# Ordering a graph by TensorE counts, with x scattered and layer 0's rows made beside the neighbour lists

## The chip, the cores and the metric

One NeuronCore of a Trainium2 chip runs the kernel as one program. The metric is the device time of a launch in microseconds (us), the median of several executions. The engines are named as the profile names them: PE is TensorE (matmul), DVE VectorE, ACT ScalarE, POOL GpSimd, SP SyncE, which here only issues DMAs. PS is the accumulator memory behind PE (eight banks of 512 floats in each of 128 partitions), `big` is one large SBUF buffer out of which nearly all tiles are cut by hand.

## What is computed

Four graph attention layers, each behind a layer norm with a relu and in front of a residual add, on x of 8 x 2048 x 64 (batch, nodes, features). The graph is sparse: a node has itself and about four neighbours on average.

```python
h = jnp.maximum(_layernorm(x, axis=-1), 0.0)
x = x + _L0_gnn_ref(h, adj, L0_gnn_W, L0_gnn_a, L0_gnn_gamma, L0_gnn_beta)
h = jnp.maximum(_layernorm(x, axis=-1), 0.0)
x = x + _L1_gnn_ref(h, adj, ...)      # 4 heads of h h^T scores, then a second attention
h = jnp.maximum(_layernorm(x, axis=-1), 0.0)
x = x + _L2_gnn_ref(h, adj, ...)      # query/key/value attention
h = jnp.maximum(_layernorm(x, axis=-1), 0.0)
x = x + _L3_gnn_ref(h, adj, L3_gnn_W, L3_gnn_a)

def _L0_gnn_ref(h, adj, W, a, gamma, beta):
    Wh = jnp.einsum('bnf,fo->bno', h, W)
    e = (Wh @ a[:Fout] + jnp.swapaxes(Wh @ a[Fout:], 1, 2)) / dk
    e = jax.nn.leaky_relu(e, negative_slope=0.2)
    attention = jax.nn.softmax(jnp.where(adj[None] > 0, e, NEG_INF), axis=2)
    h_prime = jnp.einsum('bij,bjo->bio', attention, Wh)
    # batch norm per node over batch and features, gamma, beta, then + h, then elu
```

## The kernel before

Nodes are worked in NT = 16 tiles of P = 128; a node's row holds its E = 512 numbers (8 batches of 64 features). The kernel first sorts the nodes by degree, so that a tile has as many neighbour slots as its largest node needs (SLOTS, 87 slots in all, between 2 and 13 in a tile). Every attention layer then gathers, for each tile and slot, the 128 rows of that neighbour with one indirect DMA that POOL issues (`gather`, L654, 71 a layer), and DVE, ACT and PE score, weigh and add them. If a node does not fit its slots, a flag sends all engines to another, dense program (`far_away`), which these inputs do not take; the other branch is `near`.

Everything up to the first gather is the part at issue here, and no engine's order there is set by a planner: each engine's program is written out by hand and runs in that order, with semaphores between them.

1. Masks. SP loads adj in 16 tiles into three buffers (L504). For each tile DVE writes a 0/1 mask in fp16 and its row sums, the degrees (L1489), and takes the diagonal out (L1491, L1493).
2. Ranks. DVE makes a key of degree and node number (L1497 to L1500); SP stores it and loads it back broadcast to all partitions (L507, L509). Meanwhile DVE clears and fills the weight tiles (L1502 to L1531). The rank of a node is the number of keys above its own: ACT counts for ten tiles by a sign with a running sum (L824), DVE for six by a comparison (L1535). Thirteen small operations turn ranks into places (L1542 to L1548).
3. Places. SP stores the places and loads them back broadcast (L512, L514), DVE casts them (L1558). ACT then issues the 16 loads of x (L833).
4. Lists. For each tile the mask is multiplied by the places, by POOL for 12 tiles (L638) and by DVE for four (L1568); five MAX8 and more on DVE take the largest places out as the neighbour list (L1570 to L1577). Lists, gamma, beta, bias and node number are written into the same row XR as x (547 numbers). Then the flag is made (L1587 to L1595).
5. Scatter. POOL sends the 16 tiles of XR to their places in the DRAM tensor xs by indirect DMAs (L644). SP loads lists and x back in order (L550, L552).
6. Layer 0's rows. `norm(0, s)` runs over DVE, POOL and ACT (sum and mean L1608 and L1609, centring L666, square L854, sum L1613, Ln and Exp L858 and L861, relu and scale L1617 into H0). PE turns each tile by four transposes (L1176), ACT takes it out (L845), PE multiplies it with the weights (`half`, L1196), ACT takes that out (L872), SP stores it into tab0 (L530), from which the gathers read.

In layer 0 itself the loop of m runs on each engine: `add_up` on PE adds the weighed slots of a tile (L1214), POOL gathers tile m + 2 once `summed` says that tile m - 2 is done, DVE does `weigh` (L1675), `add_terms` and `lower`, `elu_add` (L1739, L1741), `norm(1, ...)`, `elu_low` (L1732, L1733, which adds H0) and `bn_stats`.

## Time and profile before

| | us |
|---|---|
| median of 3 runs | 1794.92 (1794.16 to 1799.05) |
| the profiled execution, its own time | 1795.05 |
| its span in the profile | 1793.2 |
| busy: DVE, PE, POOL, ACT | 1308.8, 1080.2, 1035.0, 784.8 |
| mean granted clock of TensorE | 0.858 |

The granted clock is a share of full speed: 1.00 is the level of 2.4 GHz and 0.50 that of 1.2 GHz. All times within the profile count from the start of the span. A PE record of a matmul on float32 stands for half of the instruction: the 87 slot sums of a layer give 174 records, and `half` gives eight records for a tile's four matmuls, while a transpose is one record. "x16" behind an instruction is how many are merged in a row, and the text in square brackets is how long the engine had been idle and what ended it.

### The profile page before, as it was taken

Reading aid. Unit: us, or ns where it says so; the run is one execution under the profiler, and the core shown is the slowest. Engines: PE = TensorE matmul, PEld = TensorE weight load, DVE = VectorE, ACT = ScalarE, POOL = GpSimd, SP = SyncE. Lnnn points to the kernel's source line nnn. Section 1 sums busy time; section 2 is a strip of 40 time slices with the busy share of each in tenths; the row PEclk is TensorE's granted clock in tenths of the full one; section 3 lists DMA queues with packets and bytes.
Section 4 is the critical chain, followed back from the end, with each engine's and each line's share of the span. In section 5 each row is a group of like instructions: output and inputs, shape, how many; then the busy total and the mean of one; then the engine's idle time right before and its main releaser. Section 6 shows DMA issues by size and latency. Waiting matters only on the chain.

```text
span 1793.2 us, 13782 instructions
## 1 busy us (share of the span) xinstructions
PE 1080.2 (60%) x3144; PEld 558.8 (31%) x3144; DVE 1308.8 (73%) x1699; ACT 784.8 (44%) x2502; POOL 1035.0 (58%) x939
## 2 busy tenths in 40 slices
PE   0000255365289899869999985646534777764673
PEld 0000132122144444434444441212113444542231
DVE  7987456789699997994768505999976986734462
ACT  0400253334247566544655652536433546643131
POOL 0084437641167788657686656877744865415882
PEclk9999988687699899979999998877775889876886
DMA  9260547431222122101111004442204543206666
GB/s 339 74 117 20 198 153 207 136 114 48 94 62 80 41 66 64 53 12 30 42 41 36 12 12 143 131 114 84 87 24 138 149 137 96 70 34 186 199 186 160
DMA packets 101626, 178.81 MB, mean 100 GB/s; under 512 B 47552, under 2 KB 56032, under 8 KB 99232
## 3 DMA queue, kind: packets, MB, share of 16 engines
q0 software_dynamic: 30960, 102.92, 19.9%
q1 hardware_dynamic: 51216, 70.05, 11.8%
q10 hardware_dynamic: 19360, 4.87, 1.6%
q8 instruction: 28, 0.46, 0.1%
q14 instruction: 62, 0.51, 0.1%
HBM read 147.88 MB, written 34.12 MB: 101 GB/s over the span
## 4 chain that ended last, share of the span: by engine, by line
DVE 30%; PE 29%; POOL 19%; issue 11%; ACT 5%; DMA 4%; DVEq 0%; POOLq 0%; ACTq 0%; SPq 0%
PE PS L1230 15%; POOL big L654 10%; DVE big L1691 5%; DVE big L1683 3%; PE PS L1176 3%; PE PS L1254 2%; PE PS L1290 2%; ACT big L897 2%; PE PS L1242 2%; DVE big L1687 2%; DVE big L1570 2%; POOL big L682 2%; DVE big L1617 2%; DVE stats L1613 2%; DVE big L1489 2%
## 5 line engine op out<-in xcount | busy, mean ns | idle before, releaser
L1230 PE MATMUL PS<-big,ident 128*128 128x512 f32 x1044 | 507.5, 637 | 107.1 <-ACT big L897 45.2
L897 ACT ACTIVATE big<-big 128x64 f32<-128x64 f32 x1632 | 404.7, 339 | 241.8 <-DVE big L1648 202.6
L682 POOL TENSOR_TENSOR big<-big 128x512 f32<-128x512 f32 x356 | 361.5, 1045 | 134.8 <-DVE big L1648 113.0
L1230 PEld LDWEIGHTS PS<-big,ident 128*128 128x128 f32 x1044 | 209.7, 206 | 367.4 <-issue 269.4
L1691 DVE TENSOR_REDUCE big<-big 128x32 f32<-128x2048 f32 (+4 forms) x126 | 297.7, 2362 | 4.3
L1214 PE MATMUL PS<-big,ident 128*128 128x512 f32 x348 | 190.3, 708 | 153.7 <-ACT big L897 85.8
L1683 DVE TENSOR_TENSOR big<-big,PS 128x2048 f32<-128x2048 f32 (+4 forms) x84 | 198.5, 2363 | 80.9 <-PE PS L1242 78.1
L654 POOL DMA_INDIRECT big<-tab,SI x142 | 174.2, 1227 | 117.7 <-PE PS L1214 40.9
L1176 PE MATMUL PS<-ident,big 128*128 128x128 f32 x640 | 105.8, 295 | 167.8 <-DMA big<-h_rows 67.8
L689 POOL TENSOR_TENSOR big<-big 128x512 f32<-128x512 f32 x64 | 81.5, 1273 | 147.7 <-ACT big L970 147.3
L654 POOL DMA_INDIRECT big<-h_rows,SI x142 | 138.4, 974 | 44.7 <-issue 27.2
L1214 PEld LDWEIGHTS PS<-big,ident 128*128 128x128 f32 x348 | 77.3, 229 | 265.6 <-issue 232.0
L1176 PEld LDWEIGHTS PS<-ident,big 128*128 128x128 f32 x640 | 82.8, 151 | 236.3 <-DMA big<-h_rows 69.4
L1687 DVE TENSOR_TENSOR big<-big,PS 128x2048 f32<-128x2048 f32 (+4 forms) x42 | 99.3, 2363 | 68.2 <-DMA big<-h_table,SI 56.8
L666 POOL TENSOR_TENSOR big<-big,stats 128x512 f32<-128x512 f32 x64 | 66.7, 1043 | 106.4 <-DVE stats L1609 106.2
L638 POOL TENSOR_TENSOR big<-big 128x2048 f16<-128x2048 f16 x12 | 51.1, 4294 | 98.8 <-DVE big L1558 96.1
L1613 DVE TENSOR_REDUCE stats<-big 128x8 f32<-128x512 f32 x64 | 43.9, 686 | 78.8 <-ACT big L854 77.1
L879 ACT ACTIVATE big<-big 128x40 f32<-128x40 f32 (+12 forms) x80 | 20.2, 253 | 176.5 <-DVE big L1637 176.5
L1242 PE MATMUL PS<-MB,big 128*128 128x256 f32 x256 | 67.5, 411 | 34.9 <-DVE big L1683 22.3
L654 POOL DMA_INDIRECT big<-h_table,SI x71 | 70.3, 990 | 25.4 <-issue 17.7
L854 ACT ACTIVATE big<-big 128x512 f32<-128x512 f32 x64 | 40.0, 625 | 101.7 <-POOL big L666 101.7
L1675 DVE TENSOR_TENSOR big<-big 128x2048 f32<-128x2048 f32 (+6 forms) x32 | 77.7, 2428 | 1.1
(159 smaller groups left out, 1534.7 us busy)
## 6 DMA issues: line engine op xcount, KB each, us to landing
big<-in_adj SPq DMA_DIRECT2D x16, 1024.0 KB, 6.1
tab<-big SPq DMA_DIRECT2D x64, 132.0 KB, 1.8
big<-tab SPq DMA_DIRECT2D x32, 264.0 KB, 3.3
h_rows<-big SPq DMA_DIRECT2D x32, 256.0 KB, 2.0
big<-h_rows SPq DMA_DIRECT2D x32, 256.0 KB, 2.8
big<-in_x ACTq DMA_DIRECT2D x16, 256.0 KB, 5.0
big<-xs SPq DMA_DIRECT2D x4, 1024.0 KB, 9.4
h_table<-big SPq DMA_DIRECT2D x16, 256.0 KB, 2.0
```

The source lines that it names most:

```text
L654: pool.indirect_dma_start(out=rowbuf[t % NRB][:, k * w:(k + 1) * w], out_offset=None, in_=tables[u], in_offset=bass.IndirectOffsetOnAxis(a ...
L682: ins = pool.tensor_tensor(bd(wbuf[:, i % NWB, j, :]), bd(rows[:, k + j, :]), over_d(S[:, h, k + j, :], B), ALU.mult)
L689: pool.tensor_tensor(zA[:, j % 2, :], zA[:, j % 2, :], zB[:, j % 2, :], ALU.add).then_inc(z_added, 1)
L897: ins = act.activation(to, row, ACT.Copy, scale=S[:, h, k + j, b:b + 1])
L1176: mm = pe.transpose(to[:, q * P:(q + 1) * P], rows[:, q * P:(q + 1) * P], ident[:, :])
L1214: mm = pe.matmul(to.rearrange("p (b d) -> p b d", b=B), ident[:, :], rows[:, k, :].rearrange("p (b c) -> p b c", b=B)[:, :, 0:D], start=(k ...
L1230: mm = pe.matmul(to, ident[:, :], wbuf[:, i % NWB, k, :], start=(u != 2 and c == 0 and k == 0), stop=(c == len(parts) - 1 and k == n - f - 1))
L1242: mm = pe.matmul(bank(4 + 2 * hp + q // 2)[:, (q % 2) * 256:(q % 2 + 1) * 256], hTo[:, t % 2, q * P:(q + 1) * P], MB[:, 2 * hp:2 * hp + 2, ...
L1613: tell(dve.tensor_reduce(stats[:, 2, v], bd(sqn[:, n % 2, :]), AX.X, ALU.add), var_made, n + 1)
L1683: return dve.tensor_tensor(pr.rearrange("p k (q c) -> p k q c", q=4), rows.rearrange("p k (q c) -> p k q c", q=4), q_half(h // 2, h).unsqu ...
L1687: return dve.tensor_tensor(pr, rows, mine.unsqueeze(1).to_broadcast([P, n, E]), ALU.mult)
L1691: run(dve.tensor_reduce(scores(u, t)[:, h, k:k + n, :].rearrange("p k b -> p (k b)"), bd(prod[:, 0:n * E]), AX.X, ALU.add))
```

## The change

- Ranks. Each node's degree becomes a one-hot vector of NV = 32 classes (L1648 of the changed kernel, a 128 x 512 fp16 tile). PE multiplies it with ones (counts for each tile and class, L1261) and, after ACT has copied the counts, with triangle matrices (L1263, L1266), which gives the number of nodes with a larger degree or an earlier number. DVE picks each node's own (L1655, L1656). The key, its round trip through DRAM and the counting of ACT and DVE are gone. POOL and ACT make the triangles during the masks.
- Places. They are spread on a diagonal (L1666) and summed over the partitions by PE (L1270), which puts them in every partition; DVE and ACT each cast half (L1674, L912). The second round trip is gone.
- Weights. POOL clears the weight tiles, ACT copies into them, and the 16 small DVE operations for the a-terms stand behind the mask of tile 12. w_built and w_multiplied move with them.
- x. SP loads x behind adj. POOL scatters it as soon as the places are known, ahead of its share of the lists; SP loads it back in order into X, which no longer lies under the masks.
- Lists. DVE multiplies 7 tiles (0, 1, 2, 3, 6, 9, 12) and POOL 9. Lists and the rest go to a second DRAM tensor `info` in three parts (tiles 0 to 7, 8 to 13, 14 and 15), POOL issuing 8, 6 and 2 more indirect DMAs of 35 numbers a row.
- Layer 0's rows. PE turns X tile by tile (L1283), multiplies by a centring matrix (L1321), ACT squares, PE multiplies by an averaging matrix (L1327), ACT takes Ln and Exp (L952, L954), DVE multiplies (`end_row`, L1680) into H0, now with features on partitions; `half` (L1303) reads it as it is. PE and ACT do this between the places and the flag. DVE's 16 `end_row` stand among the lists, after the tiles of ROWS_ENDED.
- Layer 0. PE turns H0 back into rows for `elu_low`: four transposes for each tile, behind `add_up` of a tile two further on.
- `fold`, which never did anything, is dropped.

```diff
+DVE_RANKED = [0, 1, 2, 3, 6, 9, 12]
+POOL_RANKED = [c for c in range(NT) if c not in DVE_RANKED]
+INFO_PARTS = [(0, 8), (8, 14), (14, NT)]
+ROWS_ENDED = {6: [0], 7: [1, 2], 8: [3], 9: [4, 5], 10: [6], 11: [7], 12: [8, 9], 13: [10], 14: [11], 15: [12, 13, 14, 15]}
...
@@ sync
-            sp.wait_ge(key_made, 1)
-            sp.dma_start(keyd.rearrange("(p t) -> p t", p=P), small[:, 2, :]).then_inc(key_stored, 16)
...
+            for t in range(NT):
+                sp.dma_start(XR[:, t, :].rearrange("p (b d) -> p b d", b=B),
+                             x[:, t * P:(t + 1) * P, :].rearrange("b n d -> n b d")).then_inc(x_in, 16)
...
+            sp.wait_ge(scattered, 16 * NT)
+            for i in range(4):
+                sp.dma_start(X[:, 4 * i:4 * i + 4, :], xs.rearrange("(t p) e -> p t e", p=P)[:, 4 * i:4 * i + 4, :])\
+                  .then_inc(x_part_loaded[i], 16)
+            for t in range(NT):
+                store_halves(0, t)
+            sp.wait_ge(info_scattered, 16 * NT)
+            sp.dma_start(SI[:, :, :], info.rearrange("(t p) e -> p t e", p=P)).then_inc(info_loaded, 16)
...
@@ gpsimd
+            pool.wait_ge(place_made, 1)
+            for t in range(NT):
+                pool.wait_ge(x_in, 16 * NT)
+                pool.indirect_dma_start(out=xs, out_offset=bass.IndirectOffsetOnAxis(ap=placei[:, t:t + 1], axis=0),
+                                        in_=XR[:, t, :], in_offset=None).then_inc(scattered, 16)
...
             for i, c in enumerate(POOL_RANKED):
                 if i >= 3:
                     pool.wait_ge(ranked_used, i - 2)
                 pool.tensor_tensor(pool_ranked[i % 3], mask[:, c, :], places, ALU.mult).then_inc(ranked_made, 1)
+                if i == 5:
+                    send_info(0)
+            send_info(1)
+            send_info(2)
...
@@ scalar
+            for s in range(NT + 6):
+                if s < NT:
+                    if s >= 2:
+                        act.wait_ge(xc_made, s - 1)
+                    take_turned(xT[:, s % 2, :])
+                t = s - 1
+                if 0 <= t < NT:
+                    act.wait_ge(xc_made, t + 1)
+                    if t >= 2:
+                        act.wait_ge(xvar_made, t - 1)
+                    act.activation(sqT[:, t % 2, :], bank(C_BANK[t % 3]), ACT.Square).then_inc(xc_squared, 1)
+                t = s - 2
+                if 0 <= t < NT:
+                    act.wait_ge(xvar_made, t + 1)
+                    if t >= 4:
+                        act.wait_ge(h0_made, t - 3)
+                    act.activation(rT[:, t % 4, :], bank(7), ACT.Ln, bias=epsc[:, 0:1]).then_inc(xvar_logged, 1)
+                    act.wait_ge(xvar_logged, t + 1)
+                    act.activation(rT[:, t % 4, :], rT[:, t % 4, :], ACT.Exp, scale=-0.5).then_inc(xvar_rooted, 1)
+                halves(0, s - 5, (0, 1))
...
@@ tensor
+                t = s - 1
+                if 0 <= t < NT:
+                    pe.wait_ge(turn_freed, t + 1)
+                    if t >= 3:
+                        pe.wait_ge(h0_made, t - 2)
+                    pe.matmul(bank(C_BANK[t % 3]), centring[:, :], xT[:, t % 2, :], start=True, stop=True).then_inc(xc_made, 1)
...
+                t = s - 4
+                if 0 <= t < NT:
+                    pe.wait_ge(h0_made, t + 1)
+                    for q in range(2):
+                        half(0, t, q, H0[:, t, :])
...
+                    t = m - 3
+                    if 0 <= t < NT:
+                        if t >= 4:
+                            pe.wait_ge(elu_in, t - 3)
+                        turn(bank(4 + t % 4), H0[:, t, :]).then_inc(h0_turned, 1)
...
@@ vector
+            def end_row(t):
+                dve.wait_ge(xvar_rooted, t + 1)
+                tell(dve.scalar_tensor_tensor(H0[:, t, :], bank(C_BANK[t % 3]), 0.0, rT[:, t % 4, :], ALU.max, ALU.mult),
+                     h0_made, t + 1)
...
-                        run(dve.tensor_tensor(o, o, H0[:, t, :], ALU.add))
+                        dve.wait_ge(h0_turned, t + 1)
+                        run(dve.tensor_tensor(o, bank(4 + t % 4), o, ALU.add))
```

How instructions stand on the engines. First DVE between the weights or masks and the places, before:

```order
L1531 MEMSET small 128x16
L1535 TENSOR_SCALAR big,small<-big,small 128x2048 x6
L1539 TENSOR_SCALAR small<-small 128x10
L1542 TENSOR_SCALAR small<-small 128x16
L1546 TENSOR_SCALAR small<-small 128x16
```

and now, from the last mask on:

```order
L1626 TENSOR_TENSOR big<-big 128x128
L1646 TENSOR_SCALAR small<-small 128x16
L1648 TENSOR_TENSOR big<-small,big 128x512
L1650 COPY big<-iot 128x16
L1651 MEMSET big 128x16
L1652 MEMSET small 128x16
L1655 TENSOR_TENSOR big<-PS,big 128x512
L1656 TENSOR_REDUCE small<-big 128x16
L1658 TENSOR_SCALAR small<-small 128x16
```

Six counts over 2048 keys have become one one-hot product, one product with PE's sums and one reduction, all 512 wide; L1655 waits for PE and ACT.

Second POOL, from the constants to the first gather, before:

```order
L632 IOTA iot 128x16
L638 TENSOR_TENSOR big<-big 128x2048 [waits places_made]
L638 TENSOR_TENSOR big<-big 128x2048 x2
L638 TENSOR_TENSOR big<-big 128x2048 [waits ranked_used] x9
L796 TENSOR_LOAD flag [waits flag_made]
L796 ISA x2
L797 COMPARE_AND_BRANCH
L644 DMA xs<-big,placei 2048x547 [waits x_in,ordered]
L644 DMA xs<-big,placei 2048x547 x15
L666 TENSOR_TENSOR big<-big,stats 128x512 [waits mean_made] x16
```

and now:

```order
L680 DMA xs<-big,placei 2048x512 [waits x_in,place_made]
L680 DMA xs<-big,placei 2048x512 [waits x_in] x15
L696 TENSOR_TENSOR big<-big 128x2048 [waits places_cast,places_made]
L696 TENSOR_TENSOR big<-big 128x2048 x2
L696 TENSOR_TENSOR big<-big 128x2048 [waits ranked_used] x3
L688 DMA info<-big,placei 2048x35 [waits lists_made]
L688 DMA info<-big,placei 2048x35 x7
L696 TENSOR_TENSOR big<-big 128x2048 [waits ranked_used] x3
L688 DMA info<-big,placei 2048x35 [waits lists_made]
L688 DMA info<-big,placei 2048x35 x5
L688 DMA info<-big,placei 2048x35 [waits lists_made]
L688 DMA info<-big,placei 2048x35
```

The scatter of x stands ahead of the products and of the branch, the sixteen centrings are gone, and three parts of lists stand among and behind the products.

Third PE, one tile of layer 0's rows in the steady part, before (transposes of one tile, then `half` of the one ahead of it):

```order
L1176 MATMUL PS<-ident,big 128x128 [waits turn_freed,h_made]
L1176 MATMUL PS<-ident,big 128x128 x3
L1196 MATMUL PS<-WB,big 128x132 [waits half_staged,turn_freed]
L1196 MATMUL PS<-WB,big 128x132
L1196 MATMUL PS<-WB,big 128x132 [waits half_staged]
L1196 MATMUL PS<-WB,big 128x132
```

and now, for four tiles at once at different steps:

```order
L1283 MATMUL PS<-ident,big 128x128 [waits turn_freed]
L1283 MATMUL PS<-ident,big 128x128 x3
L1321 MATMUL PS<-big,centring 128x512 [waits h0_made,turn_freed]
L1327 MATMUL PS<-big,averaging 128x512 [waits xvar_logged,xc_squared]
L1303 MATMUL PS<-WB,big 128x132 [waits half_staged,h0_made]
L1303 MATMUL PS<-WB,big 128x132
L1303 MATMUL PS<-WB,big 128x132 [waits half_staged]
L1303 MATMUL PS<-WB,big 128x132
```

Two products of 512 columns have come between, and two waits for DVE's `end_row` (h0_made): the centring of tile t waits for row t - 3, `half` of tile t for row t.

## Rows read from the trace of the kernel before

**Rows 1.** Busy time by stretch: PE, PEld, DVE, ACT, POOL, clock, DMA, GB/s
```profile
98.00:168.00 70.00, 0.00 (x0) 0.00 (x0) 65.01 (x134) 0.00 (x0) 50.93 (x12) 1.00 0.35 57
...
204.00:254.00 50.00, 29.79 (x192) 23.88 (x192) 38.30 (x64) 33.68 (x96) 16.66 (x16) 0.99 0.39 136
```
**Rows 2.** Timeline of DVE, last mask to lists: start, duration, line, operation
```profile
56.38 0.29 DVE L1493 TENSOR_TENSOR big<-big 128x128 f16<-128x128 f16 x1
...
97.75 1.23 DVE L1568 TENSOR_TENSOR big<-big 128x2048 f16<-128x2048 f16 x1
...
119.67 2.88 DVE L1570 MAX8 big<-big 128x8 f32<-128x512 f16 x4
...
123.34 2.88 DVE L1570 MAX8 big<-big 128x8 f32<-128x512 f16 x4
...
147.66 5.10 DVE L1568 TENSOR_TENSOR big<-big 128x2048 f16<-128x2048 f16 x1
```
**Rows 3.** The chain of work that ended last, 192 to 254.3 us: start, duration, what (gather next)
```profile
192.94 2.95 DMA xs<-big,placei
...
196.33 6.97 DMA big<-xs
...
253.53 0.80 issue
```
**Rows 4.** Groups of small DVE operations, 0 to 100 us: busy us, mean ns
```profile
L1523 DVE TENSOR_TENSOR big<-WB,big 64x64 f32<-64x64 f32 x8 | 1.8, 219 | 0.3
...
L1555 DVE TENSOR_TENSOR small<-small 128x16 f32<-128x16 f32 x7 | 1.2, 175 | 0.2
```
**Rows 5.** Groups of 512-wide DVE and ACT work, 200 to 300 us: busy, mean ns
```profile
L1617 DVE SCALAR_TENSOR_TENSOR big<-big,stats 128x512 f32<-128x512 f32 x16 | 14.0, 872 | 1.0 <-ACT stats L861 0.5
...
L872 ACT ACTIVATE big<-PS 128x264 f32<-128x264 f32 x32 | 10.9, 388 | 2.1 <-DMA tab<-big 2.1
...
L845 ACT ACTIVATE big<-PS 128x512 f32<-128x512 f32 x16 | 9.3, 581 | 0.1
...
L1739 DVE SCALAR_TENSOR_TENSOR big<-big 128x512 f32<-128x512 f32 x1 | 0.7, 693 | 0.0
```
**Rows 6.** Timeline of PE, 205 to 250 us; last row: one slot-sum stretch of layer 0
```profile
213.16 2.13 PE L1196 MATMUL PS<-WB,big 128*128 128x132 f32 x8
...
219.91 0.66 PE L1176 MATMUL PS<-ident,big 128*128 128x128 f32 x4 [0.40 <-DVE big L1617]
220.94 1.17 PE L1196 MATMUL PS<-WB,big 128*128 128x132 f32 x8 [0.37 <-ACT big L845]
...
300.00:305.00 5.00, 4.89 (x12) 2.28 (x13) 1.00 0.68 183
```
**Rows 7.** Queues of SP and ACT: start, time issuing; last two: median us to landing
```profile
0.75 46.65 SPq L504 DMA_DIRECT2D big<-in_adj  x16
...
95.77 17.37 ACTq L833 DMA_DIRECT2D big<-in_x  x16
...
big<-in_x ACTq DMA_DIRECT2D x16, 256.0 KB, 5.0
...
SI<-xs SPq DMA_DIRECT2D x1, 280.0 KB, 3.6
```
**Rows 8.** POOL: its list products (ns min/median/max), and one indirect DMA of the scatter
```profile
L638 POOL TENSOR_TENSOR big<-big x12: 4042/4045/5082, 97.8 to 147.6; 128x2048 f16<-128x2048 f16 x12
...
175.12 0.96 POOL L644 DMA_INDIRECT xs<-big,placei  x1 [0.30 <-issue]
```
**Rows 9.** Timeline in layer 0: a DVE product against POOL's gather issue; PE's sums
```profile
286.00 3.36 DVE L1675 TENSOR_TENSOR big<-big 128x3072 f32<-128x3072 f32 x1
...
286.14 4.03 POOL L654 DMA_INDIRECT big<-tab,SI  x1 [0.30 <-issue]
...
342.94 8.20 PE L1214 MATMUL PS<-big,ident 128*128 128x512 f32 x12 [4.20 <-DVE big L1675]
```
**Rows 10.** Page, part 4: the chain that ended last, share of the span
```profile
DVE 30%; PE 29%; POOL 19%; issue 11%; ACT 5%; DMA 4%; DVEq 0%; POOLq 0%; ACTq 0%; SPq 0%
```

More of the change, by code:

```diff
@@ L213, in program @@
-        act_junk = take(N)
-        wload = take(16 * D)
+        take = taker(NT * E)
+        mask = take(NT * N // 2).bitcast(F16).rearrange("p (t n) -> p t n", t=NT)
+        wload = take(16 * D)
+        XR = H0
+        take = taker(wide_at + NT * E)
+        pool_ranked = [take(N // 2).bitcast(F16) for _ in range(3)]
+        dve_ranked = take(N // 2).bitcast(F16)
+        take = taker(wide_at + NT * E)
+        later = take(4 * E // 2).bitcast(F16).rearrange("p (q s) -> p q s", q=4)
+        triangle = take(2 * E).rearrange("p (i s) -> p i s", i=2)
@@ new lines, in program @@
+        before, ones16 = (take(P // 2).bitcast(F16) for _ in range(2))
+        onehot = take(E // 2).bitcast(F16)
+        counts = take(E // 2).bitcast(F16)
+        spread = take(N // 2).bitcast(F16).rearrange("p (t j) -> p t j", t=NT)
+        classes, classi = take(NV), take(NV).bitcast(I32)
+        take = taker(work_at)
+        adjt = take(3 * N).bitcast(I32).rearrange("p (s n) -> p s n", s=3)
+        places = take(N // 2).bitcast(F16)
+        lists = take(NT * NL).rearrange("p (t k) -> p t k", t=NT)
@@ L593, in far_away @@
                 sp.wait_ge(ordered, 1)
[L594 removed]
+                for i in range(NPS):
+                    sp.wait_ge(half_stored[i], 16 * (2 * NT // NPS))
                 for t in range(NT):
@@ new lines, in _ @@
+            act.wait_ge(ident_made, 2)
+            act.activation(ones16, ones, ACT.Copy).then_inc(triangle_cast, 1)
+            for q in range(5):
+                act.wait_ge(triangle_made, q + 1)
+                act.activation(before if q == 4 else later[:, q, :], triangle[:, q % 2, 0:P if q == 4 else E],
+                               ACT.Copy).then_inc(triangle_cast, 1)
+            act.wait_ge(w_in, W_LOADS)
+            act.wait_ge(w_turned, 1)
+            act.wait_ge(consts_made, 15)
@@ new lines, in _ @@
+            for q in range(4):
+                mm = pe.matmul(bank(1), counts[:, q * P:(q + 1) * P], later[:, q, :], start=False, stop=(q == 3))
+            mm.then_inc(rank_summed, 1)
+            pe.wait_ge(spread_made, 1)
+            for q in range(4):
+                mm = pe.matmul(bank(2 + q), ones16, spread[:, 4 * q:4 * q + 4, :].rearrange("p t j -> p (t j)"),
+                               start=True, stop=True)
+            mm.then_inc(places_summed, 1)
+            pe.wait_ge(w_terms, 1)
@@ new lines, in half @@
+            def half(l, t, q, hT_):
+                m = 2 * (NT * (l // 3) + t) + q
+                b = bank(4 + q) if l == 0 else bank(7)
+                if l == 0 and t >= 1:
+                    pe.wait_ge(half_staged, m - 1)
+                if l == 3:
+                    pe.wait_ge(half_staged, m)
+                for i in range(2):
+                    mm = pe.matmul(b[:, i * 2 * RW:(i + 1) * 2 * RW], hT_[:, (2 * q + i) * P:(2 * q + i + 1) * P],
+                                   blocks(WB[l][:, 0, :, :]), start=True, stop=True)
+                mm.then_inc(half_projected, 1)
```

444 lines of the change are left out of this document (219 added, 225 removed).

## The prediction

> **What bounds the kernel now.** I read the busy time by stretches first, then the chain of work that ended last, then the timelines of the single engines where the chain passes. No gather starts before 254.3 us (253.53 + 0.80 [rows 3]), 14% of the span, and what stands ahead of it runs one step after the other. In the stretch of the lists DVE is busy 65.0 of 70 us and PE and ACT do nothing; from 168 to 203.3, when the first quarter of x has landed (196.33 + 6.97 [rows 3]), DVE, PE and ACT wait for the scatter and the loading back; in the stretch of layer 0's rows DVE, ACT and PE share 50 us at 38, 34 and 30 us of work [rows 1]. So the change is about the length of this serial part, and what is saved ahead of 254.3 is saved in full, as far as the work after it stays as it is: nothing behind the first gather runs earlier than it for another reason.
>
> The profiled execution took 1795.05 us, 1.85 more than its span and 0.13 more than the median of the runs; I sum against 1795.05 and take that for the median too.
>
> **Step 1, to the first list.** Before, the last mask ends at 56.67 and the first product of the lists starts at 97.75 [rows 2]. Now:
> - Behind the mask of tile 12 come 16 small operations, at 0.219 each and some 0.03 between two [rows 4], 4.0 us, with one more copy of 0.2. DVE is the bound at that point, so they count: the masks end at 60.9. ACT's copies into the weight tiles, POOL's triangles and clearing run while both engines would be idle and cost nothing; the cover is the 40 us of masks.
> - Clamp and one-hot: 0.2 and 0.7 (512 wide, as L1739 with 0.693 [rows 5]). Then PE's four small products 0.8 with the handover, ACT's copy of 512 columns 0.58 [rows 5], and four fp16 products of 512 columns. No row shows fp16 on PE. A float32 product of 512 columns has two records of 0.41 at granted clock 1.00 (4.89 us for 12 records [rows 6]); I take one such record each, 1.7 us; between 0.8 and 3.3. Product and reduction on DVE 1.4, both 512 wide. That is 66.5.
> - Places: 14 operations of 0.175 and a gap of 0.03 [rows 4], 2.9: the places are there at 69.4.
> - Spreading them is 2048 wide in float32, 2.3 by the 3072 in 3.36 [rows 9], with a small one ahead 2.5; then 15 operations for the caps 3.1, which hide PE's four products (1.7) and ACT's half of the cast, then DVE's half, 1024 columns, 1.2 by the same ratio. The first list starts at **76.2**, 21.5 us earlier. Both round trips through DRAM are gone, and with them six counts on DVE.
>
> **Step 2, x.** SP issues x behind adj, whose issuing ends at 47.4; the 16 loads of x took ACT's queue 17.4 us [rows 7] and the last lands 5.0 after its issue [rows 7], at 70. That is level with the places (69.4), so POOL starts to scatter at 70.4; each takes 0.96 with 0.30 ahead [rows 8], 16 of them 20.2 us. Beside them DVE now spreads the places and makes three or four list products of 1.23, all with two inputs in SBUF. The row to judge that by is in layer 0: POOL's issue of one gather took 4.03 us and not 0.95, beside a DVE product of 3.36 that started 0.14 before it [rows 9]. By this row each DVE product beside the scatter delays it by up to its own length: 2.2 + 3 x 1.2 = 5.8, of which I take 5, and POOL is done at 95.7. The Trainium skill (SBUF — State Buffer, "Who interferes with whom") says that a `tensor_tensor` with two inputs in SBUF contends with GpSimd's reads, but infers that it does not hold up the writing of descriptors. By that rule the scatter would end at 90.6; the row of layer 0 speaks against it, and the row decides.
>
> Last scatter landed 2.95 later, first quarter of X 7.0 after its issue [rows 3]: 106 us.
>
> **Step 3, the lists.** A tile's list takes 3.67 (119.67 to 123.34) and DVE's own product 1.23 when nothing is in its way [rows 2]. From 76.2: 16 x 3.67 = 58.7 and 7 x 1.23 = 8.6. POOL's first product is ready at 95.7 + 4.04 [rows 8] = 99.8, when DVE has been through its four tiles since 97 or so: 2.7 of waiting. From there POOL needs 4.04 for a product where DVE needs at least 3.67 for a list and does three more products itself, so POOL stays ahead even with 8 scatters of 1.26 in between. DVE's product at 147.66 took 5.10 beside a POOL product of 4.04 that started with it [rows 2, 8]: DVE can lose 0 to 3.9 at each of tiles 3, 6, 9 and 12. I take 4 in all; bounds 0 and 12. Preparing the lists in three parts is 12 small operations, 2.6 us, before had 4 wide ones behind the lists. Thirteen `end_row`, up to that of row 12: one is 512 wide with two inputs, 0.69 at the least and 0.87 beside POOL [rows 5]; I take 0.72, 9.4 us.
>
> Are the rows ready? PE's work for a tile is 0.66 (turning) + 0.82 + 0.82 + 1.17 (`half`) [rows 6] = 3.5; ACT's is 4 x 0.6 + 2 x 0.39 [rows 5] = 3.2. X arrives at 106, the first row is through its chain at about 115, and then one every 3.6 us: row 1 at 118, row 5 at 133, row 9 at 147, row 12 at 158. DVE asks for them at 113, 119, 131, 147 and 163. So the second and the third are late by about 2 us in all, and from tile 9 on DVE is the later one. Sum: 58.7 + 8.6 + 2.7 + 4 + 2.6 + 9.4 + 2 = 88.0, so `end_row(12)` ends at **164.2**. By itself the list stretch grows from 70 [rows 1] to 88 us; that is where the rows of layer 0 now are.
>
> **Step 4, the tail.** The centring of tile 15 waits for `end_row(12)`. Behind it: centring 0.82, square 0.6, average 0.82, Ln and Exp 1.2, ACT's two copies of tile 11 in between 0.78, `end_row` 0.7, `half` 1.17, two copies 0.78, with eight handovers of 0.05: 7.3. SP then stores the last halves (0.6) and only after them issues the load of the lists, 3.6 [rows 7], then the gathers start 0.8 later [rows 3]: 12.3, and I take 12.8 with the issue. The flag is made 10 us after `end_row(12)` and is not the last. First gather at **177.0**, 77.3 us earlier than now.
>
> The last 2 scatters of lists (2.5 us, landed 3 later) end near 170, ahead of the stores. What would be late next if the tail were shorter is this load.
>
> **Step 5, layer 0.** Sixteen more turnings on PE, 0.66 each, or 1.2 at the ratio by which the `half` of 213.16, PE's first, is slower than the later ones (2.13 against 1.17 [rows 6]). They stand behind `add_up`, where PE waited 4.20 us for DVE [rows 9]; where it is busy through, a gather can wait one turning. Between 0 and 16 x 1.2 = 19 us; I take 1, since DVE and POOL hold the chain in most of layer 0. `elu_low` has one input in PS now and the same length. The sum: 1795.05 - 77.3 + 1 = 1718.8, **1719**.
>
> Bounds of the unknown terms: places 2 us earlier or 3 later, POOL's wait 0 or 6, port waits 0 or 12, rows' lateness 0 or 8, `end_row` at 0.69 or 0.87 each. Taken together without all of them at one end: 1710 to 1731 without the turnings.
>
> **The rivals.**
> - *Nothing collides.* If DVE's products and POOL's don't hold each other up, the waits of steps 2 and 3 (2.7 and 4) and the rows' lateness go: 1719 - 8 = 1711. For it: DVE's product at 97.75 took 1.23 though POOL's first started beside it, at 97.8 [rows 2, 8]. Against it: 5.10 and 4.03 [rows 2, 9]. 10%. Of these 8 us, 2.7 are what the inference of the Trainium skill on descriptors (SBUF — State Buffer, "Who interferes with whom") would give back by itself.
> - *The turnings count.* If every tile's `summed` comes one turning later and POOL's gathers with it, 12 to 19 us: 1733. Against it is that gap of 4.20, and that a turning stands behind the sum, not ahead of it. 12%.
> - *The rows are the bound.* If PE runs all of them as slowly as its first `half`, a tile costs 1.2 + 1.5 + 1.5 + 2.1 = 6.3, and row 15 comes at 115 + 15 x 6.3 = 210, the first gather some 9 later at 219: 35 us saved, 1760. It begins to count once a tile takes more than (170 - 115) / 15 = 3.7 us. Against it: in the stretch from 204 on PE was busy 30 of 50 us at granted clock 0.99 [rows 1], and here it is busy 3.5 of 3.7 to 5. 8%.
> - *Lists longer than summed*, the port waits at their upper end and a tile's row at 4.1 us: 1731. 10%.
> - *Slower than before.* PE holds 29% of the chain [rows 10], 520 us, nearly all behind the first gather, at a mean granted clock of 0.858. If the other rhythm of the start shifted the layers against the clock so that PE were granted less, the chain would grow; to eat 77 us it would have to be granted 0.858 x 520 / 597 = 0.75 in the mean. The order of work in the layers is the same, and no reason is seen why it should drop. 3%, at 1805.
>
> The change also could fail to do what it says only in one way: that `info` or x is waited for by the branch. The order shows the scatter ahead of the flag, so I leave that out.
>
> **How the numbers follow.** The forecast has 57%, at 1719 with its own range of 1711 to 1728. The range that holds 8 in 10 has to reach to 1711 and, for the turnings and the longer lists, beyond 1733; it leaves out the rows as the bound and the slow case, 11%: 1707 to 1738. A measurement of this kernel can tell about 0.3%, 5.4 us. Faster by more than that is every case but the last: 0.97; within 0.3% 0.01; slower 0.02.
>
> **What would show it.** In the profile of the changed kernel: first product of the lists at 76 (right between 73 and 80); 16 scatters of x from 70 to 96, some of them above 2 us beside DVE's products; lists, with 13 rows among them, 88 us long; first gather at 177; from first gather to the end 1539 us as before (1793.2 - 254.3), within 3. If the first gather is at 177 and the end isn't 77 earlier, step 5 is wrong. If PE's centring and averaging records take 0.8 each and not 0.4, the rows are the bound. If DVE waits for ACT's Exp at more than three `end_row`, step 3's table of readiness is wrong.

## The result, and the profile of the changed kernel

The changed kernel takes 1744.93 us (median of four runs, 1742.12 to 1747.11) where the kernel before, on the same chip, took 1796.86 (1794.16 to 1799.05). The ratio is 0.9711, 95% interval 0.9687 to 0.9734: 2.9% faster. The prediction was 1719, range 1707 to 1738. The sign was right, the gain is 52 us and not 76, and the time lies 7 us outside the range. The first gather, whose time was the sum of the prediction, starts at 202.8 us and not at 177.0. One execution of a kernel below, the one without turnings, ran in a slower state of the chip (1839.81 us at a mean granted clock of 0.754) and is left out of that kernel's median.

This is the page's head of the changed kernel: the span, then each engine's busy time and instructions, then the shares of the chain that ended last (before: [rows 10]).

```profile
span 1745.3 us, 14021 instructions
...
PE 1126.9 (65%) x3285; PEld 580.0 (33%) x3285; DVE 1276.5 (73%) x1619; ACT 786.8 (45%) x2514; POOL 1025.7 (59%) x957
...
PE 31%; DVE 27%; POOL 18%; issue 12%; ACT 6%; DMA 4%; SPq 1%; DVEq 0%; ACTq 0%; POOLq 0%
```

DVE's share of the chain went from 30 to 27% and PE's from 29 to 31%. The busy times by stretch of the changed kernel (columns as in [rows 1]) say where:

```profile
76.00:97.00 21.00, 0.00 (x0) 0.00 (x0) 18.82 (x37) 0.00 (x0) 17.32 (x14) 1.00 0.49 179
97.00:120.00 23.00, 10.40 (x32) 6.06 (x33) 21.42 (x28) 6.98 (x12) 16.34 (x5) 0.84 0.48 179
120.00:201.00 81.00, 51.05 (x228) 31.22 (x226) 51.78 (x109) 42.40 (x84) 31.81 (x20) 0.92 0.19 59
```

Up to 120 us DVE is busy nine tenths of the time, as in the list stretch before; but its 21.4 us from 97 to 120 include 8.1 in which one product stood held, as shown below. From 120 to 201 nobody is: PE 51, DVE 52, ACT 42 of 81 us. The prediction had DVE as the engine that never stops up to `end_row(12)`. Three engines at 50 to 65% suggest that they wait for each other in turn, which the waits have to show. The trace's waits from 97 to 201 us, changed kernel (who waits, for what; total us, how many, longest):

```profile
PE PS L1303 <- ACT big L933: 23.5, 13, 1.8
...
DVE big L1680 <- ACT big L954: 22.0, 10, 4.4
...
PE PS L1321 <- DVE big L1680: 12.3, 2, 8.9
```

L1303 is PE's `half`, L933 ACT's copy of a half into its staging tile, L954 ACT's Exp, L1680 DVE's `end_row`, L1321 PE's centring.

What ends the wait of each? The chain that ended last shows one turn of the ring, then the tail up to the first gather (changed kernel; start, duration, what):

```profile
175.71 1.14 PE PS L1303 x8
176.85 0.44 PE PS L1283 x4
177.29 0.86 PE PS L1321 x2
178.15 0.87 PE PS L1327 x2
...
179.04 0.70 ACT big L952
...
180.30 0.38 ACT big L933
...
180.81 1.14 PE PS L1303 x8
...
194.39 1.14 PE PS L1303 x8
...
198.08 0.40 ACT big L933
198.50 0.36 SPq L544
...
198.90 3.68 DMA SI<-info
...
202.84 5.34 DMA big<-tab,SI
```

So one turn is this. From one `half` to the next is 180.81 - 175.71 = 5.10 us. PE does `half`, turning, centring and averaging one behind the other, 3.31 us; then ACT does Ln (L952), Exp (L954) and only then the copy of the half of the tile ahead (L933); then PE's next `half` may write into the same bank. PE and ACT take turns instead of running side by side.

### The profile page after: what moved, and what is told of

Same layout as the page of the kernel before. It is cut to its first block, busy times and chain, and to the rows that moved or that the text cites. A ratio compares the mean times of both kernels' runs of the same rounds, so it can differ in the third digit from the quotient of the medians.

```text
span 1745.3 us, 14021 instructions
## 1 busy us (share of the span) xinstructions
PE 1126.9 (65%) x3285; PEld 580.0 (33%) x3285; DVE 1276.5 (73%) x1619; ACT 786.8 (45%) x2514; POOL 1025.7 (59%) x957
## 3 DMA queue, kind: packets, MB, share of 16 engines
q1 hardware_dynamic: 67280, 72.13, 13.1%
## 4 chain that ended last, share of the span: by engine, by line
PE 31%; DVE 27%; POOL 18%; issue 12%; ACT 6%; DMA 4%; SPq 1%; DVEq 0%; ACTq 0%; POOLq 0%
PE PS L1367 15%; POOL big L710 10%; DVE big L1813 6%; DVE big L1805 3%; PE PS L1283 3%; ACT big L997 3%; DVE big L1809 3%; PE PS L1391 2%; PE PS L1425 2%; PE PS L1303 2%; PE PS L1379 2%; POOL big L737 2%; DVE big L1739 1%; DVE big L1622 1%; DMA big<-in_adj 1%
## 5 line engine op out<-in xcount | busy, mean ns | idle before, releaser
L710 POOL DMA_INDIRECT big<-tab,SI x142 | 170.5, 1201 | 129.8 <-PE PS L1353 44.3
L1283 PE MATMUL PS<-ident,big 128*128 128x128 f32 x704 | 113.5, 290 | 145.2 <-DMA big<-h_rows 67.2
L1283 PEld LDWEIGHTS PS<-ident,big 128*128 128x128 f32 x704 | 90.7, 149 | 221.6 <-issue 97.2
L1379 PE MATMUL PS<-MB,big 128*128 128x256 f32 x256 | 71.9, 431 | 33.5 <-DVE big L1805 20.9
L721 POOL TENSOR_TENSOR big<-big,stats 128x512 f32<-128x512 f32 x48 | 50.1, 1044 | 70.1 <-DVE stats L1731 70.0
L1735 DVE TENSOR_REDUCE stats<-big 128x8 f32<-128x512 f32 x48 | 32.9, 686 | 77.6 <-ACT big L965 76.6
L1379 PEld LDWEIGHTS PS<-MB,big 128*128 128x128 f32 x256 | 53.2, 214 | 52.9 <-DVE big L1805 23.3
L922 ACT ACTIVATE big<-PS 128x512 f32<-128x512 f32 x64 | 37.4, 593 | 72.8 <-PE PS L1283 72.8
```

The lines of the kernel that those rows point to most:

```text
L710: pool.indirect_dma_start(out=rowbuf[t % NRB][:, k * w:(k + 1) * w], out_offset=None, in_=tables[u], in_offset=bass.IndirectOffsetOnAxis(a ...
L1283: mm = pe.transpose(to[:, q * P:(q + 1) * P], rows[:, q * P:(q + 1) * P], ident[:, :])
L1379: mm = pe.matmul(bank(4 + 2 * hp + q // 2)[:, (q % 2) * 256:(q % 2 + 1) * 256], hTo[:, t % 2, q * P:(q + 1) * P], MB[:, 2 * hp:2 * hp + 2, ...
```

## The experiments

All are made from the changed kernel. Theory A is mine after the two traces: three holds make up the difference. The ring makes a tile's row cost 5.10 us; DVE's own products wait for POOL's; and the first `end_row`, late behind such a product, holds PE. Theory B, the rival, was each time a different limit, named in what was expected.

The kernel before took 1798.97 us (median) on the chip of the first four experiments and 1794.34 on that of the last three, where it had taken 1796.86 beside the changed kernel. So times are compared by their ratios to the kernel before; a time in us that was expected can be some 2 us off by the chip alone. First gathers and waits come from one profiled execution of each kernel.

### Taking the ring apart

The copy of the halves moved from the end of ACT's step to its start:

```diff
             for s in range(NT + 6):
+                halves(0, s - 5, (0, 1))
                 if s < NT:
...
                     act.activation(rT[:, t % 4, :], rT[:, t % 4, :], ACT.Exp, scale=-0.5).then_inc(xvar_rooted, 1)
-                halves(0, s - 5, (0, 1))
```

> ACT's two copies of a tile's projections (halves) stand at the start of its loop step instead of behind Ln and Exp; nothing else differs from the changed kernel. Theory A (the row pipeline is the bound, and its cycle of 5.1 us comes from PE's half waiting 1.81 us for ACT's copy of the tile ahead): that wait goes, the cycle falls to 3.3 to 4 us, DVE's waits for ACT's Exp inside the lists (22 us with the last three rows) fall below 6, first gather at 182 to 187 instead of 202.8, time 1725 to 1730. Theory B (the product of DVE at tile 6 that was held up for 8.1 us, and the longer lists on DVE, are what cost the 26 us, and the rows only follow): the cycle may shorten but the first gather stays within 3 us of 202.8 and the time at 1742 to 1747.

Measured: 1735.72 us, ratio to before 0.9654 (0.9633 to 0.9675); first gather 187.8. This is PE's timeline in this kernel (start, duration, line, operation; in brackets the idle time ahead and what ended it). PE's `half` of two tiles in a row comes 3.05 us apart, with no wait:

```profile
134.59 1.06 PE L1303 MATMUL PS<-WB,big 128*128 128x132 f32 x8
...
137.64 1.06 PE L1303 MATMUL PS<-WB,big 128*128 128x132 f32 x8
```

The same line in the changed kernel, with the 1.81 us of waiting that stands in every turn from 133 us on:

```profile
145.09 1.14 PE L1303 MATMUL PS<-WB,big 128*128 128x132 f32 x8 [1.81 <-ACT big L933]
```

One call moved in one engine's order brings the first gather 15.0 us forward. DVE's waits for ACT's Exp fall from 22.0 to 6.8 us, and in five other turns PE now waits for DVE's `end_row` instead, 18.9 us in all. The ring is shown as a cause: theory B had the first gather within 3 us of 202.8. Theory A's own figures were all missed by a little: first gather 182 to 187, waits below 6, a turn of 3.3 to 4. The time lies between A's range and B's, 5.7 and 6.3 us away. The gain in the whole time, about 9 us by the medians and 10 by the ratios, is smaller than the 15 of the first gather; that stands below, under what stays open.

### DVE's products out of POOL's way

DVE makes its four products ahead of POOL's first one, and none between POOL's:

```diff
-DVE_RANKED = [0, 1, 2, 3, 6, 9, 12]
+DVE_RANKED = [0, 1, 2, 3]
```

> DVE multiplies only tiles 0 to 3, POOL the other twelve, so that no DVE product stands against a queue of POOL products. Theory A: end_row(0) comes 8 to 9 us earlier (118 to 109) and the row pipeline starts that much earlier, but its cycle stays 5.1 us; first gather at 193 to 197, time 1735 to 1740. Theory B: the three products and their waits (9.35 + 1.23 + 3.01 us) are the whole of what was missed, and the first gather comes 14 us or more earlier, at 189 or below, time 1731 or below.

Measured: 1744.98 us, ratio 0.9694 (0.967 to 0.9717); first gather 197.9. `end_row(0)` came 8.7 us earlier, and the whole gained nothing that can be told. DVE's timeline, this kernel:

```profile
109.46 0.69 DVE L1680 SCALAR_TENSOR_TENSOR big<-PS,big 128x512 f32<-128x512 f32 x1
...
144.01 0.69 DVE L1680 SCALAR_TENSOR_TENSOR big<-PS,big 128x512 f32<-128x512 f32 x1 [0.75 <-ACT big L954]
...
149.11 0.69 DVE L1680 SCALAR_TENSOR_TENSOR big<-PS,big 128x512 f32<-128x512 f32 x1 [0.75 <-ACT big L954]
```

The rows still come every 5.10 us. Of the 8.7 us, 4.9 are left at the first gather; most of the rest goes in one turn, where the next `end_row` came 8.11 us after the one ahead (130.80 to 138.91) and PE's records had double length, 2.10 for the eight of `half`, at a granted clock of 0.56 from 131 to 138. The ring sets the pace as long as it stands. B's sum for this kernel (first gather at 189 or earlier) fell. A's first gather was missed by 1 us and its time by 5: the 4.9 us don't show in the whole, in part because this execution took 3.5 us more behind the first gather than that of the changed kernel (1546.0 against 1542.5).

### Both together

> Both edits. Theory A: the row pipeline is no bound any more and DVE's lists are; first gather at 170 to 177, time 1713 to 1721, which is what the prediction summed. Theory B: no more than the four-product edit alone gives, within 3 us.

Measured: 1724.2 us (1722.79 to 1728.21), ratio 0.9589 (0.9567 to 0.9611); first gather 178.5. DVE's timeline of this kernel:

```profile
113.58 3.82 DVE L1703 TENSOR_SCALAR big<-big 128x128 f32<-128x128 f32 x1
...
163.09 1.42 DVE L1680 SCALAR_TENSOR_TENSOR big<-PS,big 128x512 f32<-128x512 f32 x2
```

`end_row(12)` ends at 163.8, where step 3 of the prediction had it at 164.2, and the first gather is 1.5 us behind the predicted 177.0. That both are near the prediction's figures is in part luck. DVE makes three products fewer here than the sum had (3.7 us by 1.23 each), but its `TENSOR_SCALAR` are still held (3.82 and 1.66), and it waits 4.2 us for ACT's Exp inside the lists where 2 were taken. Alone, e1 brought the first gather 15.0 us forward and e2 4.9; together 24.3, more than their sum, since the second limit shows only when the first is gone. A's range was 170 to 177 and is missed by 1.5 us, and its time (1713 to 1721) by 3.2; B, no more than the four products alone, fell. This kernel is 1.3% faster than the changed one (0.9589 against 0.9711), and it beats both.

### Turnings in layer 0

The sixteen turnings beside the sums were the prediction's other open term. Here they are left out, and DVE adds the row of H0 as it lies, so that the kernel adds the wrong layout of h:

```diff
-                    t = m - 3
-                    if 0 <= t < NT:
-                        if t >= 4:
-                            pe.wait_ge(elu_in, t - 3)
-                        turn(bank(4 + t % 4), H0[:, t, :]).then_inc(h0_turned, 1)
...
-                        dve.wait_ge(h0_turned, t + 1)
-                        run(dve.tensor_tensor(o, bank(4 + t % 4), o, ALU.add))
+                        run(dve.tensor_tensor(o, o, H0[:, t, :], ALU.add))
```

> The sixteen turnings of H0 in layer 0 are left out: PE does not turn the rows back and the elu step adds the unturned H0 from SBUF instead, so layer 0 adds the wrong layout of h. Step 5 of the prediction (turnings cost 0 to 2 us): the stretch from first gather of layer 0 to the first of layer 1 stays at 223 to 225 us (224.3 with them, 223.8 in the kernel before), time equal to the changed kernel within 3 us. Rival (turnings delay the sums that release gathers): 6 us or more faster.

Measured: 1748.95 us (median of three), ratio 0.973 (0.9706 to 0.9753); the interval overlaps with that of the changed kernel. The time is 4.0 us above the changed kernel's where equal within 3 was expected, and not below it, as the rival had it. These are the issues of POOL's gathers by source in this kernel and, below, in the changed one (ns min/median/max, first and last start):

```profile
L710 POOL DMA_INDIRECT big<-tab,SI x142: 950/957/6265, 201.4 to 1705.5; - x142
...
L710 POOL DMA_INDIRECT big<-h_rows,SI x142: 952/963/1065, 426.8 to 1499.4; - x142
```

```profile
L710 POOL DMA_INDIRECT big<-tab,SI x142: 947/953/5211, 202.8 to 1705.3; - x142
...
L710 POOL DMA_INDIRECT big<-h_rows,SI x142: 949/960/1045, 427.1 to 1500.4; - x142
```

From the first gather of `tab` to the first of `h_rows` it is 225.4 us without the turnings and 224.3 with them. They cost nothing that can be seen.

### One POOL product fewer in the queue

POOL may run only two products ahead of DVE instead of three:

```diff
-                if i >= 3:
-                    pool.wait_ge(ranked_used, i - 2)
+                if i >= 2:
+                    pool.wait_ge(ranked_used, i - 1)
```

> From the changed kernel: POOL may be two list products ahead of DVE instead of three, so that when DVE asks for its product of tile 6 at 105.1 only one more POOL product is queued behind the running one instead of two. Theory A (a DVE product waits until POOL has no product ready, however many that are): the DVE product of tile 6 takes 5.0 to 5.8 us instead of 9.35, end_row(0) comes 4 us earlier and the time is 2 to 5 us lower. Theory B (it waits for the running one only, and 9.35 has another cause, such as the transfers that land then): 9 us or more again, or 1.2 to 1.6 us.

Measured: 1744.75 us, ratio 0.9715 (0.9696 to 0.9734); first gather 199.8. In this kernel DVE's product of tile 6, and the run of POOL's products that it started in (the last column is how many stood back to back):

```profile
105.92 5.36 DVE L1691 TENSOR_TENSOR big<-big 128x2048 f16<-128x2048 f16 x1
```

```profile
94.08 16.11 POOL L696 TENSOR_TENSOR big<-big 128x2048 f16<-128x2048 f16 x4
```

And in the changed kernel:

```profile
105.09 9.35 DVE L1691 TENSOR_TENSOR big<-big 128x2048 f16<-128x2048 f16 x1
```

```profile
93.25 20.09 POOL L696 TENSOR_TENSOR big<-big 128x2048 f16<-128x2048 f16 x5
```

DVE's product ends 1.1 us behind the last of POOL's queued products in both (114.44 against 113.34, 111.28 against 110.19), whatever their number. A third run says the same: in e7, below, the product of tile 12 took 8.07 us (142.79 to 150.86) beside three POOL products in a row, busy to 149.77. So DVE doesn't lose one POOL product there but all that are ready. `end_row(0)` came 3.2 us earlier (114.97), where A had 4, and the first gather 3.0. That this is worth 2 to 5 in the whole, as A had it, is not shown: the ratios are 0.9715 and 0.9711.

### Rows asked for sooner, and rows last

With e3 as the base, DVE's list of which rows stand behind which list was drawn forward (ending with rows 14 and 15 behind the last list instead of four rows):

```diff
-ROWS_ENDED = {6: [0], 7: [1, 2], 8: [3], 9: [4, 5], 10: [6], 11: [7], 12: [8, 9], 13: [10], 14: [11], 15: [12, 13, 14, 15]}
+ROWS_ENDED = {6: [0], 7: [1], 8: [2, 3], 9: [4], 10: [5, 6], 11: [7, 8], 12: [9], 13: [10, 11], 14: [12, 13], 15: [14, 15]}
```

> Copies first and four products on DVE, as in e3, and in addition the sixteen end_row are spread as 6:0, 7:1, 8:2 3, 9:4, 10:5 6, 11:7 8, 12:9, 13:10 11, 14:12 13, 15:14 15, so that two and not four stand behind the last list. Theory A (with the copies first a row takes 3.1 to 3.5 us, and what is left of the tail is the last rows behind the last list): first gather at 170 to 175 instead of 178.5, time 1715 to 1721. Theory B (the rows can't be ready sooner, and DVE waits for them inside the lists what it saves behind): first gather within 2 us of 178.5, time 1722 to 1727.

Measured: 1720.42 us (1717.47 to 1723.69), ratio 0.9579 (0.9559 to 0.96), first gather 179.0. This is B's case by the first gather, half a microsecond from e3's, and by the ratio, which can't be told from e3's 0.9589; the time in us lies in A's range, on a chip on which the kernel before was 4.6 us faster. B's reason is not shown, though. In DVE's timeline stand a wait for a list product of POOL's and one for a row:

```profile
135.16 2.88 DVE L1693 MAX8 big<-big 128x8 f32<-128x512 f16 x4 [3.19 <-POOL big L696]
...
147.83 0.69 DVE L1680 SCALAR_TENSOR_TENSOR big<-PS,big 128x512 f32<-128x512 f32 x1 [3.21 <-ACT big L955]
```

Over all sixteen rows DVE waits less for ACT's Exp than in e3, 5.7 us against 9.8, but 6.7 for POOL's products against 2.3. And this execution was later from the start: first list product at 77.47 against 76.13, PE's first turning of X at 103.34 against 100.58. So the new order of rows gave no gain that can be seen in one execution each, and why is open.

The other way round, in the changed kernel, all rows behind the last list:

```diff
-ROWS_ENDED = {6: [0], 7: [1, 2], 8: [3], 9: [4, 5], 10: [6], 11: [7], 12: [8, 9], 13: [10], 14: [11], 15: [12, 13, 14, 15]}
+ROWS_ENDED = {15: list(range(NT))}
```

> From the changed kernel: all sixteen end_row stand behind the last list, so that the rows of layer 0 are made after the lists and not beside them; the rest as it is. Theory A (making rows beside the lists is what gave most of the gain, and a row costs 5.1 us by PE's wait for ACT's copy): lists end at 160 to 165, then 15 rows at 5.1, first gather at 240 to 250, time 1782 to 1793, that is 40 to 48 us of the changed kernel's 52 gone. Rival (ranks by counting and the early scatter gave most of it): first gather below 220, time below 1765.

Measured: 1787.92 us, ratio 0.9969 (0.9957 to 0.9981), first gather 247.5, both where A had them; the lists ended at 167.5 and not at 160 to 165, with that product of 8.07 among them. With nothing beside them the rows come at the ring's pace, 5.10 us (DVE's timeline, this kernel):

```profile
223.79 0.69 DVE L1680 SCALAR_TENSOR_TENSOR big<-PS,big 128x512 f32<-128x512 f32 x1 [4.41 <-ACT big L954]
228.89 0.69 DVE L1680 SCALAR_TENSOR_TENSOR big<-PS,big 128x512 f32<-128x512 f32 x1 [4.41 <-ACT big L954]
```

So of the 51.5 us by which the change brings the first gather forward (254.3 to 202.8), 44.7 go if the rows aren't made beside the lists. The new ranking and the earlier scatter alone are worth 6.8 here, since without the overlap their gain is eaten by the ring: sixteen rows at 5.10 cost more than the 50 us of [rows 1].

## Why the prediction was wrong

Step 5 and the frame held, but for the last microseconds. From the first gather to the end it was 1538.9 us before and is 1542.5 now, with 1 us of growth predicted and a sign of "within 3" that is missed by half a microsecond; 2.7 of the 3.6 us of growth lie in the stretch from the first gather of `h_rows` to that of `h_table` (608.1 and 610.8), which takes 607.7 to 610.8 over all the kernels here. In the stretch up to the first gather of `h_rows`, where the turnings are, it is 223.8 and 224.3. The profiled execution took 1747.1 us where 1718.8 was summed for it, 28.3 more: 25.8 of them lie ahead of the first gather (202.8 against 177.0) and 2.6 behind it. The median of the runs is another 2.2 lower.

**Step 1 held.** DVE's timeline, changed kernel (the product on the degrees, the cast of the places, the first list product and a later one):

```profile
64.70 0.69 DVE L1655 TENSOR_TENSOR big<-PS,big 128x512 f32<-128x512 f32 x1 [2.90 <-PE PS L1266]
...
69.19 0.17 DVE L1664 CAST placei<-small 128x16 int32<-128x16 f32 x1
...
76.20 1.23 DVE L1691 TENSOR_TENSOR big<-big 128x2048 f16<-128x2048 f16 x1
...
86.08 1.22 DVE L1691 TENSOR_TENSOR big<-big 128x2048 f16<-128x2048 f16 x1
```

Places at 69.4 and first product at 76.20, both as predicted. DVE waited 2.90 us for PE's degrees, where 0.8 with the handover, ACT's copy of 0.58 and 1.7 for the four fp16 products, 3.1 in all, had been summed.

**Step 2 took the holding of the scatter 4 us too dear.** POOL's timeline, changed kernel:

```profile
71.78 1.13 POOL L680 DMA_INDIRECT xs<-big,placei  x1 [48.26 <-DMA big<-in_x]
...
77.04 1.23 POOL L680 DMA_INDIRECT xs<-big,placei  x1 [0.30 <-issue]
...
86.22 1.93 POOL L680 DMA_INDIRECT xs<-big,placei  x1 [0.30 <-issue]
```

The scatter began 1.4 us later than summed, since x landed a little behind the places, and ended at 93.2 instead of 95.7; PE began to turn the first quarter of X at 100.65 and not at 106, 2.5 us by the scatter and the rest by the landing and the load, which took 7.4 behind its end where 2.95 and 7.0 were taken. Only two of the sixteen issues were held, by 0.3 and 1.0 us; I had taken 5 for four DVE products. The mechanism of [rows 9] is there: DVE's product of 86.08 ends at 87.30 and the held issue at 88.15, 0.85 later. But it holds only an issue that begins after the product: those of 81.12 and 91.00 began at the same moment as DVE's other two products and took 0.97 and 0.96. The error made the forecast too slow, and the 5 us that X came earlier bought nothing, since the first `end_row` was late for another reason. Step 3 also had a slip here: by its own figures DVE is through its four tiles at 76.2 + 4 x 4.90 = 95.8 and not at 97, so 4.0 us of waiting for POOL's first product should have stood where 2.7 did. The earlier scatter hid it; the wait was 1.9.

**Step 3 is where it failed, in two terms.** From the first list product to the end of `end_row(12)` 88.0 us were summed, and it took 105.1 (76.20 to 181.33). DVE's waits for ACT's Exp take 10.7 of them where 2 stood, what its operations lose beside POOL's 13.1 where 4 stood, and the wait for POOL's first products 1.9 where 2.7 stood: 17.0 of the 17.1 us.

The first term is the sentence on the rows: PE's 3.5 us for a tile and ACT's 3.2 were set beside each other as if the slower of them were the pace, "one every 3.6 us". They stand in one another's way. A tile's `half` writes into banks 4 and 5, the same for each tile, where the kernel before alternated between two pairs of banks (4 and 5, 6 and 7); and ACT empties them only behind Ln and Exp. The pace is PE's 3.31 plus ACT's Ln, Exp and first copy, 5.10 us. This can be read from the code with the durations of [rows 5] and [rows 6]: 3.5 for PE, 0.6 + 0.6 + 0.4 for ACT, and handovers, 5.2. The rival "the rows are the bound" had the right point from which it decides, 3.7 us for a tile, and for most of the stretch the wrong cause for passing it. It had PE slow by its clock. That is so for 16 us only: after PE had waited 8.95 us for the first `end_row`, the granted clock from 118.9 to 135 us was 0.61, and the two records of a centring took 2.05. From 140 to 190 it was 1.00, the upper level, and the centring took 1.02 with the overlap (0.87 on the chain) where 0.82 was summed; most of the turns of 5.10 lie there. The sign that the prediction set for step 3, "if DVE waits for ACT's Exp at more than three `end_row`, step 3's table of readiness is wrong", is what the trace shows: ten such waits, 22.0 us, seven of them up to `end_row(12)` and three, 11.4 us, in the tail. The sign that was set for the rival, records of 0.8 us in centring and averaging, fails in the turns of 5.10, where they take 0.44.

The second term is the port waits. DVE could lose at most 3.9 us at a product, I wrote, one POOL product's length. It lost 8.1 at tile 6 (9.35 for 1.23), and a small `TENSOR_SCALAR` behind it, 128x128, took 3.44 for some 0.2. With 1.8 at tile 12 that is 13 us, just past the 12 that I had as the bound for all, and the place mattered as well as the sum. The first `end_row` stands behind the product of tile 6 on DVE, and PE's fourth centring waits for it:

```profile
118.13 0.69 DVE L1680 SCALAR_TENSOR_TENSOR big<-PS,big 128x512 f32<-128x512 f32 x1
...
122.52 3.44 DVE L1703 TENSOR_SCALAR big<-big 128x128 f32<-128x128 f32 x1
...
139.66 0.69 DVE L1680 SCALAR_TENSOR_TENSOR big<-PS,big 128x512 f32<-128x512 f32 x1 [1.20 <-ACT big L954]
...
180.64 0.69 DVE L1680 SCALAR_TENSOR_TENSOR big<-PS,big 128x512 f32<-128x512 f32 x1
```

```profile
118.97 2.05 PE L1321 MATMUL PS<-big,centring 128*128 128x512 f32 x2 [8.95 <-DVE big L1680]
```

The sum had DVE ask for `end_row(0)` at 113, and it came at 118.1. The four rows behind it take 21.5 us, to `end_row(4)` at 139.7, with the `TENSOR_SCALAR` and PE's slow records in them. From there the ring gives the rest: eight rows at 5.10 are 40.8 us, and 139.7 + 40.8 is 180.5; `end_row(12)` starts at 180.64. It ends at 181.3 and not at 164.2: 17.1 of the 25.8 us.

The experiments say what each term is worth. With the copies first alone (e1) `end_row(12)` ends at 174.7, 6.7 us earlier; with four products on DVE as well (e3) at 163.8, another 10.9, of which 3.7 are the three products themselves. So inside the lists the held products weigh about as much as the ring, once that is gone (an estimate: 10.9 - 3.7 = 7.2 against 6.7); the ring's larger part is in the tail.

**Step 4 was 8.7 us short, by the same ring.** From `end_row(12)` to the first gather it took 202.8 - 181.3 = 21.5 where 12.8 was summed. Rows 13 and 14 come at the ring's pace behind it (`end_row` at 185.60 and 190.26, and row 15's at 194.07), and not at once. Behind the last `end_row` stand three `half` in a row (194.39, 195.65 and 196.91, 1.14 each) where one was summed; the copy, the store and the load of the lists (3.68, summed at 3.6) are as summed. With the ring gone the tail is 187.8 - 174.7 = 13.1 us in e1, near the 12.8, and 178.5 - 163.8 = 14.7 in e3. The chain of e3 shows what is more there (start, duration, what):

```profile
163.92 1.40 PE PS L1321 x2
165.33 1.72 PE PS L1327 x2
...
168.73 1.73 DMA tab<-big
```

Centring and averaging take 1.40 and 1.72 instead of 0.86 and 0.87, at a granted clock of 0.58 from 163.9 to 168, and a copy waits 1.7 us for a store out of its staging tile.

**The other rivals.** "Lists longer than summed" came nearest: it had the port waits at 12 us, which were 13.1, and a tile's row at 4.1, which was 5.10, and gave 1731. "Nothing collides" is out, by 9.35. "The turnings count" is out, by e4. "Slower than before" is out; the mean granted clock of the span went from 0.858 to 0.847, and what lies behind the first gather grew by 3.6 us of 1539.

**What stays open.** e1 gained 15.0 us at the first gather and about 9 in the medians. Most of that gap is between executions: the profiled one of the changed kernel was the slowest of its four, 2.2 us above their median, and that of e1 the fastest, 2.2 below. Between these two executions the gain is 13.6 us, and only 1.4 is lost behind the first gather (1542.5 and 1543.9). That part does vary between kernels that differ only ahead of it: up to the first gather of `h_rows` from 222.4 to 224.4 us, and from the first gather of `h_table` to the end from 703.5 (e7) over 707.4 (changed) to 712.2 (e2). Whether that is chance of one profiled execution or the rhythm of the start wasn't tried. So the times can't confirm a gain of a microsecond or two at the first gather.

## What to carry to other kernels

Where two engines hand each other the work of one tile, write down one turn of both orders with the buffers each waits for, before taking the longer of the two sums as the pace. Here a single buffer that was emptied at the end of the other engine's step, behind work that waits for the first engine, made the pace the sum of both. Put what frees a buffer at the start of the step, if its own input has long been ready. And where something new is laid beside old work, ask what is the first piece that it hands over: here a product that cost DVE 8 us at that one place held the other engine for 9.

## What the runs showed of the hardware

**A DVE product against POOL's queue.** A DVE product with two SBUF inputs that comes while POOL runs one doesn't get its turn when that POOL product ends, if the next is ready. It took 9.35 us with two more queued (POOL busy to 113.34) and 5.36 with one more (to 110.19), against 1.23 alone, and 8.07 in e7 (to 149.77). The Trainium skill (SBUF — State Buffer, "Who interferes with whom") tells of the contention between such products; that POOL's next ready products go ahead of DVE's waiting one is what these three runs add. A `TENSOR_SCALAR` with a single SBUF input is held too: the one of 128x128 took 3.44 here and 3.82 in e3, one of 128x96 took 3.42 in e5 and 0.21 in the changed kernel, with no POOL product beside it. `end_row`, with one input in PS and one in SBUF, took 0.69 in all its 16 in each run, beside POOL's products too.

**A gather's or scatter's issue against a DVE product.** The issue is held if it begins just after the product did and while it runs, and then ends 0.8 us behind the product's end, whether that took 1.2 us or 5.5. Two cases from the kernel before, each a DVE product and the issue beside it:

```profile
274.22 1.76 DVE L1675 TENSOR_TENSOR big<-big 128x1536 f32<-128x1536 f32 x1
```

```profile
274.31 2.49 POOL L654 DMA_INDIRECT big<-tab,SI  x1 [0.30 <-issue]
```

```profile
353.02 5.49 DVE L1675 TENSOR_TENSOR big<-big 128x5120 f32<-128x5120 f32 x1
```

```profile
353.94 5.39 POOL L654 DMA_INDIRECT big<-tab,SI  x1 [0.30 <-issue]
```

The products end at 275.98 and 358.51, the issues at 276.80 and 359.33, 0.82 later in both; in the changed kernel the product of 86.08 ends at 87.30 and the issue at 88.15. In the nine traces every issue that began 0.04 us or more behind such a `TENSOR_TENSOR` (of 0.69 to 5.49 us) and while it ran ended 0.82 us or more behind its end, and none that began ahead of it, or up to 0.03 us behind it, took more than 1.01. The same page of the Trainium skill infers that a `tensor_tensor` doesn't hold up the writing of descriptors. These rows differ, and they decide.
